# The last two tiles' work moved between engines and places, and one up product of tile 8

## What is computed

```
x = x + attn(layernorm(x))       # an RWKV-like block:
    r = sigmoid(xn Wr); w = -exp(xn Ww); k = xn Wk; v = xn Wv
    num = decay*num + exp(w+k)*v;  den = decay*den + exp(w+k)     # scan over the tokens
    x1 = xn + (r * num/den) Wo;    x1 + sigmoid(z Wrec) * (relu(z Wkey)^2 Wval),  z = layernorm(x1)
h = layernorm(x)
logits = h router_w.T            # 16 experts, the best one is taken, its score is sigmoid(logit)
routed = up * silu(gate) of (h * score) with the expert's weights, times its down_proj
shared = (silu(h gate.T) * (h up.T)) down.T
out = x + routed + shared
```

## Time and profile before

| | us |
|---|---|
| median of 3 runs | 487.09 (487.06 to 487.36) |
| the profiled execution's own device time | 487.54 |
| its span in the trace | 485.5 |

### The profile page before, as it was taken

The page is one execution under the profiler, slowest core; times in us unless marked ns, Lnnn a source line. Parts: engine busy times, 40 slices in busy tenths (PEclk is TensorE's granted clock), DMA queues, the critical chain, the costliest instruction groups (busy, mean ns, idle before and its releaser), DMA issues.

```text
span 485.5 us, 10435 instructions
## 1 busy us (share of the span) xinstructions
PE 474.0 (98%) x3079; PEld 385.2 (79%) x3079; DVE 370.7 (76%) x1056; ACT 323.8 (67%) x623; POOL 350.2 (72%) x573
## 2 busy tenths in 40 slices
PE   8999999999999999999999999999999999999997
PEld 7655777867778677786877867877889999999996
DVE  7889899899999998997899889837544555555426
ACT  2766887978878879787687976563255565565422
POOL 6565688898888988987688876767416777757750
PEclk9999999999999999999999999999999999999999
DMA  7007001101101011010101001011288875542027
GB/s 237 3 2 281 24 8 60 49 19 65 34 34 65 10 58 45 24 66 23 45 21 46 29 17 45 29 38 45 89 206 217 226 193 165 146 126 77 24 85 263
DMA packets 33031, 39.33 MB, mean 81 GB/s; under 512 B 4913, under 2 KB 29113, under 8 KB 32720
## 3 DMA queue, kind: packets, MB, share of 16 engines
q1 hardware_dynamic: 26640, 24.98, 18.0%
q0 software_dynamic: 5760, 13.16, 7.7%
q10 hardware_dynamic: 576, 0.52, 0.3%
HBM read 21.69 MB, written 17.93 MB: 82 GB/s over the span
## 4 chain that ended last, share of the span: by engine, by line
PE 82%; DVE 5%; POOL 5%; issue 4%; ACT 2%; DMA 1%; SPq 0%; POOLq 0%; DVEq 0%; ACTq 0%
PE bank L434 20%; PE bank L427 10%; PE bank L451 6%; PE bank L442 4%; PE bank L421 4%; PE bank L842 4%; PE bank L843 4%; PE bank L835 4%; PE bank L535 3%; PE bank L547 2%; PE bank L526 2%; PE bank L531 2%; PE bank L521 2%; PE bank L595 2%; PE bank L714 2%
## 5 line engine op out<-in xcount | busy, mean ns | idle before, releaser
L434 PE MATMUL bank<-hT,wm 128*128 128x256 f32 x512 | 124.7, 383 | 0.6 <-ACT kr L949 0.6
L434 PEld LDWEIGHTS bank<-hT,wm 128*128 128x128 f32 x512 | 92.0, 190 | 18.7 <-issue 8.3
L1569 POOL DMA_INDIRECT sorted_rows<-rows,posi x64 | 71.7, 1120 | 19.4 <-issue 17.5
L1653 POOL DMA_INDIRECT out<-shared x55 | 53.2, 966 | 36.9 <-DVE shared L1483 23.5
L427 PEld LDWEIGHTS bank<-wm,k 128*128 128x128 f32 x512 | 61.5, 192 | 7.3 <-issue 5.9
L427 PE MATMUL bank<-wm,k 128*128 128x128 f32 x512 | 62.2, 275 | 0.0
L1125 ACT ACTIVATE er<-bank 128x256 f32<-128x256 f32 x40 | 15.4, 384 | 41.2 <-PE bank L843 40.4
L1491 DVE TENSOR_TENSOR e<-er,bank 128x256 f32<-128x256 f32 x40 | 16.9, 422 | 22.6 <-ACT er L1125 18.0
L451 PE MATMUL bank<-wm,actA 128*128 128x128 f32 x240 | 32.9, 280 | 0.0
L985 ACT ACTIVATE h<-rows,smE 128x128 f32<-128x128 f32 x64 | 26.3, 482 | 7.0 <-POOL smE L1545 7.0
L451 PEld LDWEIGHTS bank<-wm,actA 128*128 128x128 f32 x240 | 29.1, 192 | 0.2 <-issue 0.2
(11 more groups left out here) (256 smaller groups left out, 1285.9 us busy)
## 6 DMA issues: line engine op xcount, KB each, us to landing
shared<-sorted_rows SPq DMA_DIRECT2D x56, 128.5 KB, 3.3
shared<-x SPq DMA_DIRECT2D x16, 256.0 KB, 2.6
rows<-sorted_rows SPq DMA_DIRECT2D x24, 128.5 KB, 3.7
wexp<-w_exp SPq DMA_DIRECT2D x2, 1536.0 KB, 9.5
sorted_rows<-filler SPq DMA_DIRECT2D x17, 128.5 KB
shared<-out SPq DMA_DIRECT2D x6, 256.0 KB, 6.6
out<-shared SPq DMA_DIRECT2D x12, 128.0 KB, 1.8
sorted_rows<-rows,posi POOLq DMA_INDIRECT x64, 2.7
```

Source lines behind the costliest of these rows:

```text
L434: ins = mm(dst[:, j * HALF:(j + 1) * HALF], W(name, 2 * pair_ + j), src[:, half * HALF:(half + 1) * HALF], start=True, stop=True)
L1569: g_.indirect_dma_start(sorted_ap, bass.IndirectOffsetOnAxis(posi[t % 3][:, g:g + 1].bitcast(U32), 0), rows[t % 3][:, g, :], None).then_in ...
L1653: g_.indirect_dma_start(out, bass.IndirectOffsetOnAxis(xr[k % RING][:, j, D:D + 1].bitcast(U32), 0), xr[k % RING][:, j, D + 1:ROW], None, ...
```

## The change

Five edits:

1. **Last h on two engines.** ACT's `norm_h` makes groups 0 and 1 of tile 15 only. DVE makes groups 2 and 3 in a new `last_h` (two instructions behind `next_region(y)` and ahead of `act0(y)`), and waits for its own completion (`const`). PE's `turn_h(15)` waits for both.
2. **Last rows on ACT.** For tile 15 POOL only makes the score; the four scalings of rows are a new `scaled` on ACT, behind `tanh_of_max(z)` and ahead of `c_silu0(y)`.
3. **Addition up.** DVE's `add_shared(y)` moves from behind `one_hot(z)` to ahead of it; PE's `ranks(z)` moves behind `c_up0(y)`.
4. **Tables.** DVE's `c_act0(y)` moves from behind `tables` to ahead of it; PE's `table_rows` moves behind `c_gate0(z)`.
5. **Tile 8.** Its second up product `hU1` moves behind the fourth output product and the projection Wr (`r_product`).

```diff
--- before.py
+++ after.py
@@ -230,7 +230,8 @@
         ACT_STORES = 4
         SP_LOADS, GP_LOADS = [0, 2, 4, 6, 8, 14], [10, 12]
         ADDED_BEHIND = {(N_LATE - 2, 1): range(0, 4), (N_LATE - 1, 0): range(4, 8), (N_LATE - 1, 1): range(8, N_LATE - 2)}
-        HALF_TILE = 5
+        HALF_TILE, CONSTS = 5, 14
+        LAST_H = CONSTS + 1
         EARLY_STATS = 3
         WARM_FIRST, WARM_BEFORE, WARM_BEHIND = 16, (8, 5), 4
         FULL_SLOTS = NTOK // P - NE
@@ -612,6 +613,8 @@
                 wait(pe, "h", t)
                 wait(pe, "hT", t - 1)
                 wait(pe, "xn1T", t + 3)
+                if t == NT - 1:
+                    pe.wait_ge(s["const_d"], LAST_H)
                 transposes(T4_B, h[t % 2], "T4")
 
             def c_up1(t):
@@ -725,16 +728,16 @@
                     mm(grp(TM_B, 1), grp(q[t % 2], 1), W("Wo"), start=True, stop=True)
                     wait(pe, "p3", t)
                     mm(grp(TM_B, 3), grp(q[t % 2], 3), W("Wo"), start=True, stop=True)
-                for t in at(5, B_TILES):
-                    wait(pe, "hT", t)
-                    wait(pe, "kr3", t + 2)
-                    unit_product(bank[5], "up", 1, hT[t % HR], 1).then_inc(s["hU1"], 1)
                 for t in at(2):
                     wait(pe, "p2", t)
                     mm(grp(TM_B, 2), grp(q[t % 2], 2), W("Wo"), start=True, stop=True).then_inc(s["TM2"], 1)
                 for t in at(1):
                     if t not in (2, 3):
                         r_product(t)
+                for t in at(5, B_TILES):
+                    wait(pe, "hT", t)
+                    wait(pe, "kr3", t + 2)
+                    unit_product(bank[5], "up", 1, hT[t % HR], 1).then_inc(s["hU1"], 1)
                 for t in at(5, B_TILES):
                     wait(pe, "hac0", t)
                     wait(pe, "base", t)
@@ -794,13 +797,13 @@
                 logits(z)
                 down_second(y)
                 c_gate0(y)
+                c_up0(y)
                 ranks(z)
-                c_up0(y)
                 c_gate1(y)
                 c_up1(y)
                 c_down(y - 1)
+                c_gate0(z)
                 table_rows()
-                c_gate0(z)
                 c_up0(z)
                 c_gate1(z)
                 c_up1(z)
@@ -981,10 +984,18 @@
             def norm_h(t):
                 wait(act_e, "pE", t)
                 wait(act_e, "T4", t - 2)
-                for g in range(G):
+                for g in range(G if t < NT - 1 else G // 2):
                     ins = af(grp(h[t % 2], g), base_of(t)[:, g, :], ACT.Identity, bias=smE[t % 3][:, 3, g:g + 1],
                              scale=smE[t % 3][:, 1, g:g + 1])
                 ins.then_inc(s["h"], 1)
+
+            def scaled(t):
+                wait(act_e, "sc", t)
+                wait(act_e, "T4", t)
+                wait_scattered(act_e, t - 3)
+                for g in range(G):
+                    ins = af(rows[t % 3][:, g, 0:D], grp(h[t % 2], g), ACT.Identity, scale=sc[t % 2][:, g:g + 1])
+                ins.then_inc(s["hs"], 1)
 
             def copy_h(t):
                 wait(act_e, "T4", t)
@@ -1089,6 +1100,7 @@
                 silu1(y)
                 copy_h(z)
                 tanh_of_max(z)
+                scaled(z)
                 c_silu0(y)
                 c_silu1(y)
                 c_copy(y - 1)
@@ -1241,6 +1253,15 @@
                 v.tensor_scalar(smA[0][:, 2, :], mvA[0][:, :, 1], 1.0 + LN_EPS, LN_EPS * LN_EPS, ALU.mult, ALU.add).then_inc(s["var0"], 1)
                 v.tensor_scalar(smA[0][:, 0, :], mvA[0][:, :, 0], -1.0, 0.0, ALU.mult, ALU.add).then_inc(s["var0"], 1)
                 v.tensor_scalar(smA[0][:, 1, :], mvA[0][:, :, 1], 1.0, LN_EPS, ALU.mult, ALU.add).then_inc(s["var0"], 1)
+
+            def last_h(t):
+                wait(dve, "pE", t)
+                wait(dve, "T4", t - 2)
+                for g in range(G // 2, G):
+                    ins = v.tensor_scalar(grp(h[t % 2], g), base_of(t)[:, g, :], mvE[t % 3][:, g, 0:1], smE[t % 3][:, 1, g:g + 1],
+                                          ALU.subtract, ALU.mult)
+                const(ins)
+                assert nconst[0] == LAST_H
 
             def places(t):
                 wait(dve, "posf", t)
@@ -1429,16 +1450,17 @@
                 ranked(y)
                 places(y)
                 next_region(y)
+                last_h(z)
                 act0(y)
                 act1(y)
                 largest(z)
+                add_shared(y)
                 one_hot(z)
-                add_shared(y)
                 ranked(z)
                 places(z)
                 next_region(z)
+                c_act0(y)
                 tables()
-                c_act0(y)
                 row_tables()
                 c_act1(y)
                 c_act0(z)
@@ -1548,6 +1570,8 @@
                 wait(gp, "ths", t)
                 wait(gp, "hs", t - 2)
                 g_.tensor_scalar(sc[t % 2][:, :], ths[t % 2][:, :], 0.5, 0.5, ALU.mult, ALU.add).then_inc(s["sc"], 1)
+                if t == NT - 1:
+                    return
                 wait(gp, "sc", t)
                 wait(gp, "h", t)
                 wait_scattered(gp, t - 3)
```

## The result

| | before | with the change |
|---|---|---|
| median of 12 runs, us | 487.18 | 488.35 |
| lowest to highest, us | 486.55 to 488.20 | 488.13 to 489.13 |
| profiled execution, us | 487.54 | 488.21 |
| its span, us | 485.5 | 486.4 |

A forecast was written before the change was run, and what follows sets the result against it. PE's order, busy for 98% of the span, was taken as the bound, racing a chain of POOL and DMA. -0.76 - 0.72 + 2.37 - 1.02 = -0.13 from 487.09 gave about 487.0 us, range 485.8 to 488.3.

The forecast's parts named there:

- four terms: PE's time at tile 8, last h, tables and first transposes: -0.76, -0.72, +2.37 and -1.02, sum -0.13 us.
- slow clock: Rival: after the long table stall PE runs as slowly as at program start, +2.7 us, 489.7; chance 0.13.
- tile 8: PE's stall on ACT's read of bank 5 in tile 8's round goes: -0.76 us.
- last h: PE's wait before the transposes of h of tile 15 goes: -0.72 us.
- addition, ranks, rows: Addition earlier, ranks later on PE, tile 15's row scalings on ACT: zero on PE for addition and ranks.
- tables: `c_act0(y)` ahead of the tables on DVE makes PE stand still 3.23 us in place of 0.86: +2.37 us.
- first transposes: At the slots' first transposes PE comes later and the loads earlier, so the wait is gone: -1.02 us.
- The rival in which its stall only moves: Another wait in tile 8's round takes the stall's place, 0.76 us not gained: 487.7 us; chance 0.08.
- the rival that the tables do not hold PE: The table stall stays at 0.86 us, since the change frees POOL's chain: -2.5 us, 484.6; chance 0.12.

The follow-up runs named there:

- e2_tile8_only: The kernel before with only tile 8's second up product moved; 486.33 us, ratio 0.9981.
- e4_tables_only: The kernel before with only `c_act0(y)` put ahead of the tables and the table product behind `c_gate0(z)`; 489.99 us, ratio 1.0059.
- e7_edits_1_to_3: The changed kernel with the table product back ahead of `c_gate0(z)` and `c_act0(y)` back behind the tables; tile 8's move stays in; 485.54 us, ratio 0.9966.
- e5_product_behind_up: The changed kernel with the table product one unit product later, behind `c_up0(z)`; 487.01 us, ratio 1.0003.
- e8_last_h_only: The kernel before with only the last h split over ACT and DVE; 485.93 us, ratio 0.9978.
- e6_tables_and_two_gates: The changed kernel with DVE's order tables, `c_act0(y)`, `c_act1(y)`, `row_tables`, and both gate products ahead of the table product on PE; 485.06 us, ratio 0.9954.

## Why the prediction was wrong

The forecast was a sum of four terms for "no change", with the slow clock as a rival at 0.13. The four terms held to 0.4 us each; the rival came on top, at half the price that I had put on it. In the profiled executions, from start to start, but for tile 8, which is taken from medians:

| term of the prediction | predicted | measured | how |
|---|---|---|---|
| tile 8 | -0.76 | -0.77 | e2_tile8_only, 486.33 - 487.10; in the traces 2.17 for 3.00 us, -0.83 |
| last h | -0.72 | -0.63 | unit products (328.18 before, 327.24 after) to transposes: 5.28 for 5.91 us |
| addition, ranks, rows | 0 | -0.09 | transposes to down product: 6.45 for 6.54 us |
| tables | +2.37 | +2.00 | stall 2.86 for 0.86 us |
| first transposes | -1.02 | -0.78 | to the next product: 0.46 for 1.24 us |
| sum | -0.13 | -0.27 | |
| slow clock | (rival, +2.7) | +1.39 | table product to down product, one gate product allowed for: 4.43 for 3.04 us |
| all | | +1.12 | medians: +1.17 |

Counted in the two traces alone, the first product behind the slots' first transposes starts at 354.94 for 353.98, 0.96 us later; the last rounds began 0.94 us earlier (tile 8, and 0.11 that no edit explains), and the five terms from there on add up to the rest.

- **The step that failed** is the one at which the long stall was costed as time standing still alone. I had the stall itself, its place, its cause and its length to 0.4 us; I took it as the likeliest case that PE would resume at full rate, because stalls of 0.9 us had left the clock full, which says nothing of one of 3 us. It did not: the granted clock fell to 1.2 GHz within the stall, and PE ran slowly behind it. I had this as a rival and gave it 0.13. The experiment with matmuls in the stall shows this term by itself. This is what the Trainium skill warned of, "TensorE: Matmul & The Clock Gate", section "Why this matters for your kernels": a gap between bursts of matmuls can put PE back to half its clock. The trace agrees: the clock read 0.51 behind the gap.
- **The price of the rival** was too high. I took it from the 32 matmuls at the program's start (2.7 us lost). In the middle of the program PE had work in the slow stretch for about 3 us (344.48 to near 347.5), and at half rate that costs about 1.5 us, an estimate; 1.39 was measured. Where the clock fell later, in e4_tables_only, it cost 1.78.
- **The tables** took 3.59 us to the 15th step (340.83 to 344.42) and not 3.85. That is 0.26 of the 0.37 between +2.37 and +2.00; the other 0.11 is that the tables started 0.60 us after `c_act0(y)` did and not 0.71. The lag of 1.26 us of `c_act0(y)` behind its down product, and with it the whole queue on DVE, came as worked out.
- **The first transposes** lost 0.27 us again between the down product and the first pair (352.43 + 1.78 = 354.21 to 354.48), although the loads were early. I had taken the whole 1.02 as gone. This part is 0.27 in every trace here, with a load in the way or without, and what it waits for no run shows. Only the 0.75 on the second pair was the load.
- **Tile 8** was right in mechanism and size. The rival in which its stall only moves is out.
- **The addition, the ranks and the rows on ACT** cost PE nothing up to the down product, as said. But the later ranks make the tables start later, and I had put that at nothing without a look at it. In the changed kernel `c_act0(y)` holds the tables longer still and hides it; in e7_edits_1_to_3 it makes the stall 0.71 us longer.

As to the rival that the tables do not hold PE, the trace before had the chain of waits running through POOL. The change freed that chain (its last scatter goes 2.2 us earlier), and in the changed kernel PE had no use for it: e4_tables_only, where the last scatter goes at 344.80, does not wait for the load either. Only with the tables first does it count: there PE comes to the first transposes at 351.34, and meets no wait where before it waited for the load until 353.71.

## What to carry to other kernels

Where a chain of many tiny dependent instructions feeds the engine that bounds the kernel, an instruction put ahead of it must not itself wait: what counts is when its last input comes, not its own 0.69 us. Before a consumer is moved up, work out from the trace when the buffer it writes comes free. And price a new long stall of TensorE twice, once for the time it stands still and once for the slow stretch that may follow, with its chance; where the stall can't be removed, matmuls into a free bank can fill it: ten of them kept the clock here in 11 runs of 11. And read the clock of every run, not of the profiled one alone: a median over runs with and without the slow stretch describes neither.

## What the hardware showed that I had not expected

- In the same place of the same program, stalls of about the same length do not always end the same way. By the mean clock of each run it fell in 12 of 12 runs with a stall of 2.86 us (the changed kernel), in 4 of 6 with 2.79 (e4_tables_only), in 5 of 12 with 1.99 (e5_product_behind_up) and in 0 of 5 with 1.57 (e7_edits_1_to_3). The stall lengths are those of the profiled executions, and e4_tables_only ran on another chip than e5_product_behind_up and e7_edits_1_to_3. No length below which the clock is safe follows from this, only that it fell more often behind the longer stalls.
- The clock was low 0.4 us before PE resumed in the changed kernel and fell 0.7 us after it in e4_tables_only, so the cost of nearly the same stall differs: +1.39 and +1.78 us.
- The start of the program varies from run to run. The 32 first matmuls begin at 1.8 us in every trace, and the transposes behind them at 8.05 us in the profile of before but at 7.26 in that of e8_last_h_only and at 8.38 in that of e6_tables_and_two_gates. The granted clock reads 1.00 there in all three, while 10 records start between 2 and 4 us, 0.2 us each where 0.111 is the later rate. So the recorded clock does not account for this slow stretch. A difference of 0.8 us or more between two profiles can come from there alone, which is why stages are compared from start to start.
- Scaling a 128x128 group with `scaled` on ACT took 1.28 us for four, with `norm_h`, which adds a bias, 1.65 us for four. I had counted 1.65 for both. Their tiles differ too, so that the bias is the reason is not shown.
